# The expert phase of a MoE kernel: four pairs of experts, with the middle two in a loop or written out

## What is computed

```python
scores = (jnp.tanh(xf @ gate_w.T) + 1.0) * 0.5
vals, idx = jax.lax.top_k(scores.T, k)          # k = 8224 // 8 = 1028
y = xf[flat_idx].reshape(k, n, d)
y = _layernorm(y, ln_gamma, ln_beta)
h = jnp.einsum('knd,nfd->knf', y, fc1s) + b1s   # 256 -> 1024
h = jax.nn.gelu(h, approximate=True)
o = jnp.einsum('knf,ndf->knd', h, fc2s) + b2s   # 1024 -> 256
o = o * kept_w[:, :, None]
out = xf.at[flat_idx].add(o.reshape(k * n, d))
```

## Time and profile before

| | |
|---|---|
| median of 3 runs | 784.48 us (784.38 to 785.78) |
| profiled execution | 786.62 us, span 784.8 us |
| mean granted PE clock | 0.944 |
| expert phase | about 348 to 785 us |
| busy share PE / DVE / ACT / POOL | 89 / 69 / 59 / 60% |

### The profile page before, as it was taken

How to read it: one execution, slowest core, us unless ns; L and a number is a source line. 1 busy time by engine, 2 the same in 40 slices (tenths; PEclk the granted TensorE clock), 3 DMA queues, 4 the chain that set the end, 5 groups by cost and what they waited for, 6 DMA issues and landing times.

```text
span 784.8 us, 15827 instructions
## 1 busy us (share of the span) xinstructions
PE 696.7 (89%) x4630; PEld 635.5 (81%) x4630; DVE 541.0 (69%) x1885; ACT 459.9 (59%) x1095; POOL 473.3 (60%) x660
## 2 busy tenths in 40 slices
PE   6987999999999945447999999989999999999994
PEld 3986888888888734336989999989889999899993
DVE  3765798998899778987784766756846757634431
ACT  1003588888888869315556656665566566656551
POOL 0258689888988545142366485584674855846523
PEclk9989999999999975559999999999999999999997
DMA  9900022222222228121134243352342432533222
GB/s 258 307 18 1 4 83 81 80 80 81 80 80 81 81 93 170 54 56 61 30 81 117 42 109 89 50 149 43 75 122 41 108 88 42 146 52 49 35 28 27
DMA packets 63563, 64.14 MB, mean 82 GB/s; under 512 B 14032, under 2 KB 57104, under 8 KB 63376
## 3 DMA queue, kind: packets, MB, share of 16 engines
q1 hardware_dynamic: 50576, 46.33, 19.6%
q0 software_dynamic: 12800, 17.12, 13.5%
q10 hardware_dynamic: 128, 0.00, 0.0%
HBM read 37.90 MB, written 25.53 MB: 81 GB/s over the span
## 4 chain that ended last, share of the span: by engine, by line
PE 36%; DVE 7%; issue 6%; ACT 6%; POOL 5%; DMA 3%; POOLq 0%; ACTq 0%; DVEq 0%; SPq 0%
PE bank L1022 16%; PE bank L1036 15%; ACT bank L746 2%; PE bank L1011 2%; PE bank L1048 2%; POOL out L577 2%; POOL w2l L536 1%; POOL yg L555 1%; DMA raw<-in_fc1T 1%; DMA yg<-rows,idx 1%; DVE yl L1583 1%; ACT bank L756 1%; PE bank L1001 1%; DVE jk L1560 1%; ACT hh L759 1%
## 5 line engine op out<-in xcount | busy, mean ns | idle before, releaser
L577 POOL DMA_INDIRECT out<-ob,sidx x72 | 113.9, 1582 | 160.5 <-ACT ob L772 148.8
L1590 DVE TENSOR_TENSOR hl<-bank,hh 128x384 fp32r<-128x384 f32 (+1 forms) x192 | 97.5, 513 | 139.1 <-ACT hh L759 138.6
L756 ACT ACTIVATE bank<-bank,b1s 128x384 f32<-128x384 f32 (+1 forms) x192 | 99.4, 518 | 138.0 <-PE bank L1022 133.5
L1022 PE MATMUL bank<-yh,w1h 128*128 128x384 f32 (+1 forms) x384 | 132.7, 346 | 8.1 <-DVE hl L1590 4.7
L1022 PE MATMUL bank<-yh,w1l 128*128 128x384 f32 (+1 forms) x384 | 123.8, 322 | 0.0
L1022 PE MATMUL bank<-yl,w1h 128*128 128x384 f32 (+1 forms) x384 | 123.3, 321 | 0.0
L1036 PE MATMUL bank<-w2h,hh 128*128 128x256 f32 x384 | 108.1, 281 | 0.0
L1036 PE MATMUL bank<-w2l,hh 128*128 128x256 f32 x384 | 108.0, 281 | 0.0
L1036 PE MATMUL bank<-w2h,hl 128*128 128x256 f32 x384 | 107.9, 281 | 0.0
L555 POOL DMA_INDIRECT yg<-rows,idx x72 | 72.4, 1006 | 44.2 <-issue 39.1
L759 ACT ACTIVATE hh<-bank 128x384 fp32r<-128x384 f32 (+1 forms) x192 | 87.7, 457 | 6.1
(11 more groups left out here) (249 smaller groups left out, 1770.6 us busy)
## 6 DMA issues: line engine op xcount, KB each, us to landing
BIG<-in_x SPq DMA_DIRECT2D x4, 2048.0 KB, 16.3
out<-Bs SPq DMA_DIRECT2D x32, 256.0 KB, 2.2
rows<-Yp SPq DMA_DIRECT2D x32, 256.0 KB, 2.4
raw<-in_fc1T SPq DMA_DIRECT2D x16, 512.0 KB
raw<-in_fc2T SPq DMA_DIRECT2D x16, 512.0 KB
yg<-rows,idx POOLq DMA_INDIRECT x72, 2.8
out<-ob,sidx POOLq DMA_INDIRECT x72, 3.8
gwb<-in_gate_w SPq DMA_DIRECT2D x1, 1024.0 KB, 7.2
```

The costliest lines, as they stand in the source:

```text
L577: g.indirect_dma_start(out=out_rows, out_offset=tok(ap=sidx[job.eh][0:m, t:t + 1], axis=0), in_=ob[t % 3][0:m, :], in_offset=None, compute ...
L756: A.activation(h[:, 0:cur.w], h[:, 0:cur.w], ACT.Gelu_apprx_tanh, bias=b1s[:, bass.ds(cur.e, 1), f]).then_inc(s["hact"], 1)
L1022: last = T.matmul(Lb[ring(cur, f)][:, 0:cur.w], w1s[cur.eh][i][:, d, f * P:(f + 1) * P], yT[cur.p][k][:, d, 0:cur.w], start=(n == 0), stop ...
L1590: v.tensor_tensor(hT[cur.p][1][:, f, 0:cur.w], Lb[ring(cur, f)][:, 0:cur.w], hT[cur.p][0][:, f, 0:cur.w], ALU.subtract).then_inc(s["hlo"], 1)
```

## The change

In `jobs`, which all four of PE, DVE, ACT and POOL call, the pairs 0 to 3 are now all written out with a Python number for `el`; the loop over pairs 1 and 2 is gone. No tile, no semaphore, no size and no order of operations is changed. SP's program is untouched.

```diff
-            for k in range(6):
-                one(0, k)
-            with eng.Fori(1, 3) as el:
+            for el in range(4):
                 for k in range(6):
                     one(el, k)
-            for k in range(6):
-                one(3, k)
             emit(Job(3, 5), None, None, [])
```

## The result

The changed kernel took 790.53 us (median of 5 runs, 788.67 to 790.89) against 785.78 us for the kernel before in 5 runs (784.38 to 786.82): a ratio of 1.0051, 95% interval [1.0035, 1.0067]. It is slower by 0.5%, and above the stated range. The profiled execution took 790.53 us, for a span of 788.7.

A forecast was written before the change was run, and what follows sets the result against it. PE, busy 89% of the span, was taken as the bound, with 2.27 us on offer. Terms -0.56 - 0.28 + 0.43 gave -0.4 us; the median of 784.48, shifted likewise, gave 784.1 us, range 782.6 to 785.6.

The forecast's parts named there:

- The slow landings: Late weight transfers for experts 2 and 6, loaded in q3 and q4: laid to addresses, 0; bound -1.3 us.
- What the written-out code adds: PE's 6 extra code blocks beside weight transfers, 0.15 us, plus ACT's moved block edges, +0.28: +0.43 us.
- rival 3: PE's extra code blocks collide with the second half of W1, up to 1.1 us a hit: 786.4 us, chance 0.10.
- The pause in the loop body: PE's 0.40 us idle before the placement matmul in q3 and q5 goes when ACT is written out: -0.56 us.
- Register work: PE's register operations in the loop become constants, shortening the wait for yl over four experts: -0.28 us.
- ACT's block edges: ACT's code block edges fall elsewhere, in q4 and q6; one taken as uncovered: +0.28 us, bounds 0 and 0.56.
- The back edge: The loop's one jump, ahead of q4: ACT 2.4 us late but hidden by the wait for weights, 0.

The follow-up runs named there:

- e8: The kernel before with one unused megabyte ahead of expert 0 in each weight array, so all weights lie 1 MB further on; 786.75 us, ratio 1.0012.
- e4: The kernel before with the attention phase's image loop written out on PE alone, the experts' loop kept on every engine; 787.80 us, ratio 1.0028.
- e13: The changed kernel with every expert's weights at 4 MB steps plus 512 KB, code blocks left where they are; 787.66 us, ratio 1.0025.
- e7: The changed kernel with the table of rows in device memory 928 KB longer; 789.68 us, ratio 1.0059.
- e5: The changed kernel with 64 tiny matmuls on PE after the image phase, so later code blocks are fetched sooner; 787.13 us, ratio 1.0018.
- e2: The kernel before with the experts' loop written out on DVE, ACT and POOL, PE keeping its loop; 785.30 us, ratio 0.9990.
- e1: The kernel before with the experts' loop written out on PE alone, the other three keeping theirs; 790.91 us, ratio 1.0066.
- e9: e2 with every expert's weights at 4 MB steps plus 1 MB; 784.40 us, ratio 0.9978 to the kernel before.
- e12: e5 with every expert's weights at 4 MB steps plus 512 KB; 784.38 us, ratio 0.9978 to the kernel before.

## Why the prediction was wrong

Two terms failed: the placing of the weights, put at 0, and the code blocks, put at 0.15 us. A third part is luck: the forecast of 784.1 us stood on a median of 784.48 from three runs, and the same kernel gave 785.78 in the next five, above the range as it was stated. That is 1.3 of the 6.4 us by which it was off.

- **The slow landings** ("belonging to the addresses, not to the loop: 0"). The reading was right, and `e8` shows it, though late landings were not found "only between 508 and 615 us": expert 4's halves, loaded in q0, took 3.3 to 3.4 us too. The step that failed is the one behind it: that the addresses stay where they are. With the longer code of PE the weights lie half a megabyte further on. That this code takes room in device memory ahead of them is the reading that fits; no run shows the addresses. The term was 0; against the kernel before, whose experts were half fast, it measures 1.96 us (`e4`), and against one with all experts fast 2.75 us (787.13 - 784.38). The bound had only a gain (-1.3 us), none for a loss, although the same argument, different addresses, goes both ways.
- **What the written-out code adds** ("But a block can sit before a piece of the weight transfer", 0.15 us in all). The mechanism was rival 3's, with its place and nearly its price: 1.1 us a hit was forecast, 0.7 to 1.4 are seen in q3 to q5 of `e13`. The error is in the count. It was taken as a matter of luck. But the blocks come at fixed places in the code, and they drift slowly: the first ones of the changed kernel come 7.2, 7.1, 9.9, 9.9, 10.2 and 12.3 us into q1 to q6. So where one hits, the next ones are close to it too. Four hits, with the lower clock, make 3.3 us in `e13` (787.66 - 784.38); with slow landings it is 2.55 us (789.68 - 787.13, `e7` against `e5`). The lower clock behind a long wait was in no term. The places could have been counted from the program; "q1 to q3 have them and show no such wait" was read from blocks that came at 7 us, before the transfer.
- **The pause in the loop body** (-0.56 us). Right: the gap before the placement matmul in q3 is 0.11 us (561.00 + 0.28 = 561.28 to 561.39 in the rows below), and the 0.8 us of L1001's waits are gone. `e2`, in which ACT is written out, shows it too; in `e1`, where ACT keeps its loop, the 0.4 is still there in q5.
- **Register work** (-0.28 us). Right in direction and size: the wait for yl is 0.34 to 0.35 us in q3 to q5, 0.43 before.
- **ACT's block edges** (+0.28 us). Not seen: in none of q1 to q5 does PE idle for 0.2 us or more anywhere but at the three waits of the first third.
- **The back edge** (0). Right. ACT's first GELU of q4 comes 563.84 - 562.41 = 1.43 us into the expert and no longer 3.85, and q4's time did not fall. The clean case is `e2`, in which ACT has no jump and the landings are as before: q4 takes 52.77 us against 52.81. The Trainium skill (Runtime: NRT & Kernel Launch, Instruction fetch mechanics) prefers full unrolling for such stalls; the stall was there, hidden, and here unrolling PE cost more than it could give. The same section of the Trainium skill has it that streaming a long program is mostly hidden. For PE the traces agree (it never idles for code), but the transfers that share the DMA engines with its blocks did pay, 0.7 to 1.3 us each in `e13`.

The placement in q3 of the changed kernel and ACT's first GELU of q4:

```profile
561.00 0.28 PE L1032 MATMUL bank<-w2h,hl 128*128 128x256 f32 x1
561.39 0.27 PE L997 MATMUL bank<-TB,oh 128*4 128x260 bf16 x1
```

```profile
563.84 0.55 ACT L752 ACTIVATE bank<-bank,b1s 128x384 f32<-128x384 f32 x1
```

What stays open: why the step is half a megabyte and which buffer makes it, and why a 1 MB zone in 2 MB is read faster by 0.5 us per 512 KB. Whether a whole megabyte must be inside it, or only its edges count, was not tried in finer steps than 256 KB.

## What to carry to other kernels

Code is data that moves: writing out a loop on PE adds 16 KB transfers to the DMA engines at fixed places (one for every 255 instructions of the changed kernel's q1 to q7 on average, weight load and matmul counted as two), and here a longer program of PE moved both weight arrays. Before unrolling, ask which transfer ends last and whether a block of code will fall on it; write out the engines with short code and leave the one with long code in its loop (`e2`, and `e9` with the weights placed, 0.22% faster than the kernel before). And before believing a difference of half a percent, compare the landing times of the same transfer in both traces: where those differ for code that was not touched, the placing of the buffers has changed, and the comparison must be made again with the placing fixed.

## What was unexpected in the hardware

- Two megabytes of device memory are not alike: 512 KB of weights landed 2.8 us after the issue from one megabyte and 3.2 us or more from the next, for the same experts in every run of a program, single late ones aside.
- A longer program of one engine moved both weight arrays by 512 KB against these zones (modulo 2 MB); longer programs of the three others did not (they grew by 76, 91 and 50 instructions, PE's by 657, a matmul counted once).
- A single 16 KB code packet delayed a 512 KB transfer by 0.7 to 1.3 us (`e13` against `e12`, q3 to q6), about what such a packet takes by itself on average: 32 packets took 0.3% of 16 engines' 788.7 us, 1.2 us each.
- ACT's GELU came 0.3 us late at the same instruction of both passes (0.67 us of idle time against 0.35), and ACT idled 2.3 us after the one jump back, though PE had begun the last of the matmuls that this GELU reads at 562.69 us, 3 us before it started.
- After a wait of 2.04 us PE's clock was at the lower level from 686.3 to 689.7 us (0.59 and 0.56 of full speed over the two stretches of 2 us); after one of 2.20 us in the expert before it was not.
